# Attention in units of one head pair and 512 queries, with the weighing of two half steps issued together

## The chip, the cores and the metric

The kernel runs on one core of one Trainium2 chip. The metric is the device time of one execution in microseconds (us). TensorE (PE) multiplies matrices into PSUM, VectorE (DVE) and ScalarE (ACT) read and write PSUM and SBUF, GpSimd (POOL) works on SBUF, SyncE (SP) mostly issues DMAs. Each engine works through its own instructions in order and meets the others at semaphores.

## The reference, cut to what matters

The program is two transformer layers on x of 4 x 1024 x 256: a state-space mixer, a mixture of experts with top 2 of 8, an attention, and a gated feed-forward part with blockwise fp4 quantisation, each followed by a layer norm. The change touches only the attention of the second layer:

```python
qkv = (zn @ W_qkv + b_qkv).reshape(b, n, 3, H, DH)     # b=4, n=1024, H=16, DH=16
scores = jnp.einsum('bhqd,bhkd->bhqk', q, k) * scale   # 1024 x 1024 for each of 16 heads
attn = jax.nn.softmax(scores, axis=-1)
msa = jnp.einsum('bhqk,bhkd->bhqd', attn, v)
```

## The kernel before, in words

The first part of the program (mixer, experts) takes some 470 us. After it a function `sequence(b, more)` on every engine does attention, projection and feed-forward of one batch entry, four times, with the first steps of entry b+1 laid into the end of entry b.

Attention works on pairs of heads (NP = 8 pairs; the two heads of a pair, a = 0 and 1, sit on partitions 0.. and 64.. of `Qs` and `Ks`, so that their matmuls address different rows of the PE array). The scores are computed twice, in float32r from split high and low parts:

- **For the maxima.** `score_max(n)` (L976) is one matmul of 48 rows, 128 queries by 512 keys, into one PSUM bank; DVE's `row_maxima` (L1536) reduces the bank to a maximum for each query. A pair takes UN = 32 such units (8 query tiles, 2 key halves, 2 heads). Banks: six take turns in the first UN units of an entry, afterwards only the three banks 4, 5, 6, and a unit waits on `sld` until the previous user of its bank has been read. When a pair's 32 units are reduced, DVE's `negated_maxima` makes the negated maxima, split in two (three small operations, L1540 to L1542), PE turns them (`turn_max`, L983, in a bank slot of its own), DVE copies them to `MR` (L1549), and SP sends them by two DMAs (`maxima_row`, L440) to two extra rows of `Qs` (flow `mrow`). These rows, against rows of ones in `Ks`, subtract the maximum inside the second product. `turn_slot(p)` puts the turn SOON = 1 unit (first pair) or LATER = 4 units after the pair's last.
- **For the weights.** A half step n is one key tile (128 keys) and 512 queries of both heads: `transposed_scores` (L1006, two matmuls of 50 rows by 512 columns into two banks), ACT's exponential to `Pb` (L708), and `weigh` (L1019, four fp32 matmuls with 32 output columns each, eight matmul instructions, accumulating in bank 7). A step m = (pair, key tile kt) holds the half steps qh = 0 and 1; an entry has 64 steps, 128 half steps. After a pair ACT copies bank 7 out (`evac_o`, L681; flow `ov` frees the bank).

PE's order is written out by hand. It issues the 32 units of the first pair, between them the eight `values` products (L960) with the filler matmuls of `keep_warm` (L1028), 25 further fillers, the turn, and six units of the second pair (START = 6). Then comes the loop over m. In it `maxima(upto)` keeps the units ahead of the half steps: `ahead = UN + min(LEAD + 4*m, START + 5*m)`, that is five units a step for the first steps and then four. For steps 12 to 52 (`apart`) each half step is

```python
maxima(ahead + 2 * qh + 1)
transposed_scores(p, kt, qh)
maxima(ahead + (2 if not qh else step if apart else 3))
if apart:
    weigh(m - 1, qh)
```

so one `weigh` stands behind each half step. In the steps before 12 and from 53 (LAST) on, the two `weigh` of a step stand together behind its second half step; in the steps before 12 one unit follows them, and from 53 on no units are left.

SP sends the stacked high and low parts of a pair (`stack(p)`, twelve DMAs, L432; flow `stk`) and the rows of maxima in one fixed order: stacks 0, 1, 2, row 0, stack 3, then row p-3 and stack p for p = 4 to 7, then the last rows. After the last unit DVE goes on to sums for the following stage (`combine` of the next entry), and reads the heads' results (`rc`, L1586) when PE has turned them.

Of the kernel before, what the change touches and what calls it, by code (L numbers as in the profile page):

```python
# [7 lines left out]
F32 = mybir.dt.float32  # L8
# [24 lines left out]
LEAD, START = 12, 6  # L33
# [49 lines left out]
def transformer(nc, xT, state_cols, WtT, WbT, Wc4, WoT, Dv, bo, sel, Wg, W1, b1, W2, b2, rev,  # L83
                lnw_d, lnb_d, Wqkv, bqkv_d, Wproj, bproj, w_gate, w_up, w_down, ident_d, out):
    ctx = ExitStack()
    with ctx:
# [90 lines left out]
        NM = sb("NM", [P, 2, TT])  # L177
        NMs = sb("NMs", [P, 2, 2, TT], F32R)
        MR = sb("MR", [4 * TT, 2, P], F32R)
# [58 lines left out]
        def h_dram(name, shape):  # L238
# [20 lines left out]
        UN = 2 * TT * 2  # L259
        SLOTS = NP * UN + NP  # L260
# [4 lines left out]
            qkp=8, qka=8, qkv=8, vp=TT, vv=TT, **{f"stk{k}": NP // NB * STK - (0 if k else KST) for k in range(NB)}, kst=KST, mrow=16 * 2 * NP,  # L265
            slp=SLOTS, sld=SLOTS, nms=NP,
# [6 lines left out]
        CHAIN, AHEAD = 132, 13  # L273
# [12 lines left out]
        def turn_slot(p):  # L286

            if p + 1 == NP:
                return SLOTS - 1
            return UN * (p + 1) + (LATER if p else SOON) + p  # L290

        def slot_bank(i):

            return (4, 5, 6, 0, 1, 2)[i % 6] if i < UN else 4 + (i - UN) % 3

# [42 lines left out]
        def _(sp):  # L338
# [76 lines left out]
            for b in range(B):  # L415
# [18 lines left out]
                def maxima_row(p):  # L434
                    F["sld"].wait(sp, b, turn_slot(p) + 1)
                    if p >= NB:
                        F["bp"].wait(sp, b, 2 * KT * (p - NB + 1))
                    for a in range(2):
                        r, at = ROW * a + STACK, 2 * a * TT
                        F["mrow"].inc(sp.dma_start(  # L440
                            Qs[r:r + 2, p % NB, :].rearrange("o (t q) -> o t q", t=TT).bitcast(F32),
                            MR[at:at + 2 * TT, p % 2, :].bitcast(F32)), by=16)
# [8 lines left out]
                for p in range(NP - NB + 1, NP):  # L451
                    maxima_row(p)
# [113 lines left out]
        def _(act):  # L566
# [110 lines left out]
            def sequence(b, more):  # L677
# [23 lines left out]
                for p in range(NP):  # L701
                    for kt in range(KT):
                        for qh in range(2):
                            n = 2 * (KT * p + kt) + qh
                            F["bp"].wait(act, b, n + 1)
                            if n >= 4:
                                F["pv"].wait(act, b, n - 3)
                            F["ex"].inc(act.activation(Pb[:, kt % 2, 2 * qh:2 * qh + 2, :],  # L708
                                                       PS[:, 2 * qh:2 * qh + 2, :], ACT.Exp, scale=0.25))
                            if kt == 0 and p > 0 and qh == 0:  # L710
                                evac_o(p - 1)
# [74 lines left out]
        def _(pe):  # L786
# [163 lines left out]
            def sequence(b, more):  # L950
# [13 lines left out]
                def score_max(n):  # L964

                    p, r = n // UN, n % UN
# [12 lines left out]
                def turn_max(p):  # L979
                    i = turn_slot(p)  # L980
                    F["nms"].wait(pe, b, p + 1)
                    F["sld"].wait(pe, b, slot_free(i))
                    F["slp"].inc(pe.transpose(PS[0:4 * TT, slot_bank(i), 0:P],  # L983
                                              NMs[:, :, :, :].rearrange("p a k t -> p (a k t)").bitcast(F32), ident[:, :]))
# [3 lines left out]
                def maxima(upto):  # L988

                    while issued[0] < min(upto, NP * UN):  # L990
# [8 lines left out]
                def transposed_scores(p, kt, qh):  # L999

                    n = 2 * (KT * p + kt) + qh
                    if n >= 2:
                        F["ex"].wait(pe, b, n - 1)
                    for a in (1, 0):
                        rows = slice(ROW * a, ROW * a + MROWS)
                        ins = pe.matmul(PS[:, 2 * qh + a, :], Ks[rows, p % NB, kt * P:(kt + 1) * P],  # L1006
# [3 lines left out]
                def weigh(m, qh):  # L1010

                    p, kt = m // KT, m % KT
                    if kt == 0 and p:
                        F["ov"].wait(pe, b, p)
                    F["ex"].wait(pe, b, 2 * m + qh + 1)
                    for c in range(2):
                        for a in range(2):
                            j = 2 * a + c
                            ins = pe.matmul(PS[32 * j:32 * j + 32, 7, qh * QW:(qh + 1) * QW], V[:, kt, 2 * p + a, :],  # L1019
                                            Pb[:, kt % 2, 2 * qh + a, c * QW:(c + 1) * QW],  # L1020
                                            start=(kt == 0 and qh == 0), stop=(kt == KT - 1), skip_group_check=True)
# [7 lines left out]

                maxima(3)  # L1030
# [18 lines left out]
                FIRST = 12  # L1049
                LAST = (NP * UN - UN - LEAD) // 4  # L1050
                for m in range(NP * KT):
                    p, kt = m // KT, m % KT
                    if kt == 0:
                        F["mrow"].wait(pe, b, 16 * 2 * (p + 1))
                    ahead = UN + min(LEAD + 4 * m, START + 5 * m)
                    step = UN + min(LEAD + 4 * (m + 1), START + 5 * (m + 1)) - ahead
                    apart = FIRST <= m < LAST
                    for qh in range(2):
                        if apart:
                            maxima(ahead + 2 * qh + 1)  # L1060
                        transposed_scores(p, kt, qh)
                        maxima(ahead + (2 if not qh else step if apart else 3))
                        if apart:
                            weigh(m - 1, qh)
                    if not apart:
                        for qh in range(2 if m else 0):
                            weigh(m - 1, qh)
                        maxima(ahead + step)
                        if m == LAST:
                            turn_max(NP - 1)  # L1070
                for qh in range(2):
                    weigh(NP * KT - 1, qh)
# [115 lines left out]
        def _(dve):  # L1188
# [307 lines left out]
            def sequence(b, more):  # L1496
# [33 lines left out]
                def row_maxima(lo, hi):  # L1530
                    for n in range(lo, hi):
                        p, r = n // UN, n % UN
# [5 lines left out]
                def negated_maxima(p):  # L1538
                    F["sld"].wait(dve, b, unit_slot(UN * (p + 1) - 1) + 1)
                    link(dve.tensor_reduce(NM[:, :, :], MX[:, p % 2, :, :, :], AX.X, ALU.max, negate=True))  # L1540
# [3 lines left out]
                def maxima_rows(p):  # L1544
                    i = turn_slot(p)
                    F["slp"].wait(dve, b, i + 1)
                    if p >= 2:
                        F["mrow"].wait(dve, b, 16 * 2 * (p - 1))
                    F["sld"].inc(dve.tensor_copy(MR[:, p % 2, :], PS[0:4 * TT, slot_bank(i), 0:P]))  # L1549

                row_maxima(0, UN)
                for p in range(NP):
                    negated_maxima(p)
                    gap = LATER if p else SOON
                    if p + 1 < NP:
# [170 lines left out]
```

How the kernel before makes its waits and increments, by code:

```python
    def wait(self, eng, b, n, ahead=0):  # L65
        eng.wait_ge(self.sem, b * self.per + (ahead * self.per + n))
# [12 lines left out]
    def wait(self, eng, n):  # L79
        eng.wait_ge(self.sem, n)
# [256 lines left out]
        @block.sync  # L337
# [18 lines left out]
            load(lnw[:, :], lnw_d, s_late)  # L356
            load(lnb[:, :], lnb_d, s_late)
            load(wqkv[:, :, :], Wqkv.rearrange("(c p) n -> p c n", p=P), s_late)
            load(bqkv[:, :], bqkv_d, s_late)
            load(wproj[:, :, :], Wproj.rearrange("(c p) n -> p c n", p=P), s_late)
            load(bproj_sb[:, :], bproj.to_broadcast([P, D]), s_late)
            def load_ffn(w, src):
                sp.dma_start(WN[w], src.rearrange("(t p) k -> p t k", p=WP if w < 2 else P)).then_inc(s_wld[w], 16)
            for b in range(B):
                sp.wait_ge(C["xn"].sem, TT * (b + 1))
                C[f"mid{b % 2}"].inc(sp.dma_start(x_mid[b * S:(b + 1) * S, :].rearrange("(t p) d -> p t d", p=P), Xa[b % 2]), by=16)
            sp.wait_ge(C["tab"].sem, 1)
            def load_w1(k):
                e = sp.value_load(tab[0:1, k:k + 1], min_val=0, max_val=E - 1)
                if k >= 2:
                    sp.wait_ge(C["wl"].sem, k - 1)
                C["w1a" if k % 2 == 0 else "w1b"].inc(sp.dma_start(
                    W1t[k % 2], W1[bass.ds(e, 1), :, :].rearrange("o (c p) n -> p (o c) n", p=P)), by=16)
                return e
# [1 line left out]
            def load_w2(k, e):  # L378
                if k >= 2:
                    sp.wait_ge(C["yp"].sem, SA * (k - 1))
                if k == 0:
```

## Time and profile before

| | |
|---|---|
| time of three runs | 1770.61 us median (1768.52 to 1770.95) |
| span of the profiled execution | 1760.0 us |
| median of the runs less that span | 10.6 us |
| busy: PE, DVE, ACT, POOL | 91%, 76%, 50%, 15% |
| mean granted TensorE clock | 0.948 |
| costliest groups | L1536 DVE 635.3 us, L708 ACT 511.1, L976 PE 389.8, L1006 PE 341.0, L1019 PE 319.0 |
| attention of one entry, first reduction to last copy of bank 7 | 196.5 to 199.3 us, four times |

The profile comes from one further execution; its total device time is not listed apart from its span, so the time outside the span is taken from the median of the runs. Matmuls are pipelined and overlap, so a PE that is busy in the profile is not PE at its peak, and a group's busy time counts overlaps twice. The granted clock is 1.00 (2.4 GHz) or 0.50 (1.2 GHz); a value between the two in a stretch is a mixture of both in time.

### The profile page before, as it was taken

How to read it: one execution, taken by the hardware profiler on the slowest of the kernel's cores; microseconds unless marked ns; L12 is line 12 of the kernel's file. 1: busy time of each engine (PE TensorE's matmuls, PEld its weight loads, DVE VectorE, ACT ScalarE, POOL GpSimd, SP SyncE). 2: the span in 40 equal slices, each digit the busy share in tenths (PEclk: the TensorE clock that was granted, in tenths of full speed). 3: DMA queues.
4: the chain of work that ended last, by engine and by line, in shares of the span. 5: the costliest groups of instructions: out<-in, count | busy, mean ns of one | idle time of the engine just before them, and what ended most of it. 6: DMA issues, size and time to landing. Idle time of an engine off the chain costs nothing.

```text
span 1760.0 us, 27981 instructions
## 1 busy us (share of the span) xinstructions
PE 1597.9 (91%) x10698; PEld 962.5 (55%) x10698; DVE 1345.8 (76%) x2629; ACT 875.5 (50%) x1294; POOL 258.6 (15%) x255
## 2 busy tenths in 40 slices
PE   5988999994799998899999989999997999999895
PEld 2757899994343336565433556543345754333664
DVE  3675555542589996888999689889968987996686
ACT  1313444441347784252677624367782344778412
POOL 0144223223100120210003030100203010000120
PEclk8988999997789999998999989999999998999998
DMA  3127878774312310013222000412300032210000
GB/s 134 48 72 220 253 250 257 247 235 146 60 27 36 71 38 1 1 25 73 38 38 74 2 0 1 89 27 39 80 14 1 1 78 36 36 24 2 1 0 24
DMA packets 80175, 123.03 MB, mean 70 GB/s; under 512 B 13530, under 2 KB 55771, under 8 KB 80043
## 3 DMA queue, kind: packets, MB, share of 16 engines
q1 hardware_dynamic: 70666, 93.46, 20.5%
q0 software_dynamic: 9376, 27.80, 5.4%
q8 instruction: 85, 1.39, 0.3%
q14 instruction: 48, 0.39, 0.1%
HBM read 76.84 MB, written 18.61 MB: 54 GB/s over the span
## 4 chain that ended last, share of the span: by engine, by line
PE 76%; DVE 13%; ACT 4%; issue 3%; DMA 1%; POOL 1%; SPq 1%; DVEq 0%; ACTq 0%; POOLq 0%
PE PS L1019 15%; PE PS L976 13%; PE PS L901 7%; PE PS L1131 7%; PE PS L889 6%; PE PS L1006 6%; PE PS L1141 5%; DVE MX L1536 3%; PE PS L946 3%; PE PS L960 2%; ACT Pb L708 2%; PE PS L839 2%; PE PS L1028 1%; PE PS L1090 1%; PE PS L1167 1%
## 5 line engine op out<-in xcount | busy, mean ns | idle before, releaser
L1536 DVE TENSOR_REDUCE MX<-PS 128x1 f32<-128x512 f32 x1024 | 635.3, 683 | 43.2 <-PE PS L976 41.2
L708 ACT ACTIVATE Pb<-PS 128x1024 f32<-128x1024 f32 x512 | 511.1, 1026 | 174.7 <-PE PS L1006 174.5
L976 PE MATMUL PS<-Ks,Qs 48*128 48x512 f32 x1024 | 389.8, 472 | 7.1 <-DVE MX L1536 4.3
L1006 PE MATMUL PS<-Qs,Ks 50*128 50x512 f32 x1024 | 341.0, 464 | 14.3 <-ACT Pb L708 11.5
L1019 PE MATMUL PS<-Pb,V 128*32 128x256 f32 x4096 | 319.0, 401 | 1.0
L976 PEld LDWEIGHTS PS<-Ks,Qs 48*128 48x128 f32 x1024 | 163.6, 191 | 218.8 <-DVE MX L1536 174.4
L1019 PEld LDWEIGHTS PS<-Pb,V 128*32 128x32 f32 x4096 | 92.3, 110 | 163.2 <-ACT Pb L708 84.5
L1006 PEld LDWEIGHTS PS<-Qs,Ks 50*128 50x128 f32 x1024 | 140.2, 191 | 49.7 <-ACT Pb L708 36.1
L901 PE MATMUL PS<-Pb,OT 128*128 128x256 f32 x624 | 141.0, 379 | 0.0
L889 PE MATMUL PS<-Ks,Qs 128*128 128x256 f32 x936 | 127.5, 294 | 6.4 <-DVE Ks L1416 6.4
L889 PEld LDWEIGHTS PS<-Ks,Qs 128*128 128x128 f32 x936 | 119.7, 197 | 8.9 <-DVE Ks L1416 7.8
L901 PEld LDWEIGHTS PS<-Pb,OT 128*128 128x128 f32 x624 | 115.6, 190 | 14.2
L1131 PE MATMUL PS<-wgT,XT 128*128 128x352 f32 x256 | 95.8, 525 | 15.3 <-DVE OT L1634 12.3
L473 POOL DMA_INDIRECT OT<-x_mid,idx x78 | 79.5, 1020 | 197.8 <-PE PS L878 160.0
L621 ACT ACTIVATE Qs<-Pb 128x1024 fp32r<-128x1024 f32 x39 | 41.3, 1060 | 121.3 <-DMA Pb<-W 121.3
L1141 PE MATMUL PS<-wdT,Pb 128*128 128x256 f32 (+1 forms) x384 | 96.2, 393 | 2.0 <-ACT Pb L761 2.0
L1141 PEld LDWEIGHTS PS<-wdT,Pb 128*128 128x128 f32 (+1 forms) x384 | 70.8, 192 | 26.9 <-issue 11.6
L632 ACT ACTIVATE OT<-PS,b1t 128x256 f32<-128x256 f32 x156 | 64.7, 470 | 38.2 <-PE PS L889 38.0
L1131 PE MATMUL PS<-wuT,XT 128*128 128x352 f32 x256 | 81.1, 460 | 0.0
L1131 PEld LDWEIGHTS PS<-wgT,XT 128*128 128x128 f32 x256 | 53.1, 218 | 43.6 <-DVE OT L1634 13.3
L738 ACT ACTIVATE OT<-PS 128x704 f32<-128x704 f32 x32 | 24.2, 756 | 103.4 <-PE PS L1131 103.4
L1412 DVE TENSOR_TENSOR Qs<-Pb,Qs 128x1024 fp32r<-128x1024 f32 x39 | 47.7, 1224 | 30.3 <-ACT Qs L621 29.9
(286 smaller groups left out, 1893.9 us busy)
## 6 DMA issues: line engine op xcount, KB each, us to landing
Pb<-W SPq DMA_DIRECT2D x78, 512.0 KB, 4.3
y_slot<-V SPq DMA_DIRECT2D x39, 256.0 KB, 3.9
Qs<-Qh SPq DMA_DIRECT2D x128, 64.0 KB, 2.3
Ks<-Kh SPq DMA_DIRECT2D x120, 64.0 KB, 2.3
V<-b SPq DMA_DIRECT2D x39, 128.0 KB, 3.5
XT<-x_mid POOLq DMA_DIRECT2D x4, 1024.0 KB, 6.2
out<-Pb POOLq DMA_DIRECT2D x4, 1024.0 KB, 6.7
OT<-xT SPq DMA_DIRECT2D x2, 1024.0 KB, 6.4
```

The costliest lines, as they stand in the source:

```text
L473: C[("xa", "xb", "xc")[k % 3]].inc(pool.indirect_dma_start(Xm[k % 3][:, a, :], None, x_mid[:, :], bass.IndirectOffsetOnAxis(idx[:, SA * k ...
L632: C["hr"].inc(act.activation(HTm[k % 2][:, hc, :], PS[:, 2 + 2 * (k % 2) + hc // 2, hc % 2 * ST:(hc % 2 + 1) * ST], ACT.Relu, bias=b1t[:, ...
L708: F["ex"].inc(act.activation(Pb[:, kt % 2, 2 * qh:2 * qh + 2, :], PS[:, 2 * qh:2 * qh + 2, :], ACT.Exp, scale=0.25))
L889: ins = pe.matmul(PS[:, 2 + 2 * (k % 2) + hc // 2, hc % 2 * ST:(hc % 2 + 1) * ST], w[k % 2][:, c, hc * P:(hc + 1) * P], x[k % 2][:, c, :], ...
L901: ins = pe.matmul(PS[:, 6 + k % 2, a * D:(a + 1) * D], HTm[k % 2][:, hc, a * P:(a + 1) * P], W2t[k % 2][:, hc, :], start=(hc == 0), stop=( ...
L946: ins = pe.matmul(o, wqkv[:, kc, w * D + c * P:w * D + (c + 1) * P], tokens, start=(kc == 0), stop=(kc == DC - 1))
L976: F["slp"].inc(pe.matmul(PS[:, slot_bank(i), :], Qs[rows, p % NB, t * P:(t + 1) * P], Ks[rows, p % NB, kh * HALF:(kh + 1) * HALF], start=T ...
L1006: ins = pe.matmul(PS[:, 2 * qh + a, :], Ks[rows, p % NB, kt * P:(kt + 1) * P], Qs[rows, p % NB, qh * HALF:(qh + 1) * HALF], start=True, st ...
L1019: ins = pe.matmul(PS[32 * j:32 * j + 32, 7, qh * QW:(qh + 1) * QW], V[:, kt, 2 * p + a, :], Pb[:, kt % 2, 2 * qh + a, c * QW:(c + 1) * QW] ...
L1131: ins = pe.matmul(PS[:, 2 * w + a, 0:IH], XT[:, c, t * P:(t + 1) * P], wT[:, c, a * IH:(a + 1) * IH], start=(c == 0), stop=(c == DC - 1))
L1141: ins = pe.matmul(PS[:, 6 + t % 2, 0:D], HT[0:k, c, :], wdT[0:k, c, :], start=(c == 0), stop=(c == IC - 1))
L1536: F["sld"].inc(dve.tensor_reduce(MX[:, p % 2, a, t, kh:kh + 1], PS[:, slot_bank(i), :], AX.X, ALU.max))
```

## The change

The unit of work becomes one pair and one half of the queries. UN falls from 32 to 16 and there are NU = 16 such groups u = (pair, qh). Negated maxima, turn, copy and the DMAs of the rows are done for each u, on half as many elements. `mrow` becomes two flows, one for each half. The half steps run in the order pair, query half, key tile: n = 8u + kt, so the first half step needs the maxima of 16 units only. The filler matmuls are fewer: none between the first `values` and few after them, but three times two (`fill`) behind the first three half steps. START is 8. The loop runs over half steps; each issues one unit ahead of the second product and the rest behind it, and the `weigh` of half steps n-3 and n-2 stand together behind every odd n. The last rows' turn stands ahead of half step LAST + 2. ACT copies bank 7 out behind the exponential n % 16 == 1 instead of n % 16 == 0. DVE's chain of small operations grows by 16 links an entry.

```diff
-LEAD, START = 12, 6
+LEAD, START = 12, 8
-        UN = 2 * TT * 2
-        SLOTS = NP * UN + NP
+        UN = 2 * TT
+        NU = 2 * NP
+        QT = TT // 2
+        SLOTS = NU * UN + NU
...
-                for p in range(NB - 1):
+                stack(0)
+                stack(1)
+                maxima_row(0)
+                for p in range(2, NB):
                     stack(p)
-                maxima_row(0)
-                stack(NB - 1)
+                    maxima_row(p - 1)
                 for p in range(NB, NP):
-                    maxima_row(p - NB + 1)
+                    for u in range(2 * (p - NB) + NB - 1, 2 * (p - NB) + NB + 1):
+                        maxima_row(u)
                     stack(p)
...
+                for n in range(NU * KT):                                  # ACT
+                    F["bp"].wait(act, b, n + 1)
+                    if n >= 4:
+                        F["pv"].wait(act, b, n - 3)
+                    F["ex"].inc(act.activation(weights_of(n), PS[:, 2 * (n % 2):2 * (n % 2) + 2, :], ACT.Exp, scale=0.25))
+                    if n > 2 and n % (2 * KT) == 1:
+                        evac_o(n // (2 * KT) - 1)
...
-                for t in range(1, TT):                                    # PE
-                    maxima(4 * t + 1)
-                    F["vv"].wait(pe, b, t)
-                    keep_warm(2, 1)
-                    maxima(4 * t + 3)
+                for t in range(1, 5):
+                    maxima(3 * t + 3)
                     values(t)
                 maxima(UN)
+                for t in (5, 6):
+                    values(t)
+                maxima(UN + SOON)
+                values(7)
                 F["vv"].wait(pe, b, TT)
-                keep_warm(18)
-                maxima(UN + SOON)
-                keep_warm(7, 1)
+                keep_warm(2, 1)
                 for n in range(SOON, START):
                     maxima(UN + n + 1)
                     keep_warm(3, (n + 1) % 2)
...
+                ahead = lambda n: UN + min(LEAD + 2 * n, START + 5 * n // 2)
+                LAST = (NU * UN - UN - LEAD) // 2
+                for n in range(NU * KT):
+                    if n == LAST + 2:
+                        turn_max(NU - 1)
+                    maxima(ahead(n) + 1)
+                    transposed_scores(n)
+                    maxima(ahead(n + 1))
+                    if n < 3:
+                        fill(2)
+                    elif n % 2:
+                        weigh(n - 3)
+                        weigh(n - 2)
+                for n in range(NU * KT - 2, NU * KT):
+                    weigh(n)
...
+                for u in range(NU):                                       # DVE
+                    negated_maxima(u)
+                    gap = LATER if u else SOON
+                    if u + 1 < NU:
+                        row_maxima(UN * (u + 1), UN * (u + 1) + gap)
+                    maxima_rows(u)
+                    if u + 1 < NU:
+                        row_maxima(UN * (u + 1) + gap, UN * (u + 2))
```

## Rows read from the trace of the kernel before

**Rows 1.** Windows of the four attentions, reductions alone: stretch; length, busy (count), clock, DMA
```profile
472.94:671.05 198.11, 158.84 (x256) 0.97 0.22 44
793.13:992.43 199.30, 158.83 (x256) 0.96 0.23 48
1116.20:1312.70 196.50, 158.77 (x256) 0.97 0.23 49
1434.78:1633.94 199.16, 158.81 (x256) 0.96 0.18 33
```

**Rows 2.** Chain of waits, two weigh together: start, duration, engine and line
```profile
522.56 1.00 PE PS L1019 x16
523.56 0.44 PE PS L976
524.02 0.70 DVE MX L1536
524.77 0.50 PE PS L976
525.27 1.00 PE PS L1019 x16
```

**Rows 3.** Chain of waits, one weigh behind each half step
```profile
560.15 0.57 PE PS L1019 x8
560.72 0.43 PE PS L976
561.14 0.24 PE PS L1006 x2
```

**Rows 4.** Timeline of the second entry's start: start, duration, instruction [idle before <-releaser]
```profile
799.09 1.13 PE L960 MATMUL PS<-wqkv,XT 128*128 128x256 f32 x4
...
812.39 0.19 DVE L1540 TENSOR_REDUCE NM<-MX 128x16 f32<-128x32 f32 x1
...
812.91 0.68 DVE L1536 TENSOR_REDUCE MX<-PS 128x1 f32<-128x512 f32 x1
...
813.43 0.29 PE L983 MATMUL PS<-ident,NMs 128*32 128x128 f32 x1
...
814.18 3.08 DVE L1536 TENSOR_REDUCE MX<-PS 128x1 f32<-128x512 f32 x5
...
816.87 0.50 PE L1006 MATMUL PS<-Qs,Ks 50*128 50x512 f32 x2 [0.62 <-DMA Qs<-MR]
```

**Rows 5.** Timeline at a pair's end with two weigh together
```profile
529.03 0.60 ACT L681 ACTIVATE OT<-PS 128x512 f32<-128x512 f32 x1 [1.04 <-PE PS L1019]
```

**Rows 6.** Windows of PE behind the first second products: length, busy (count), clock, DMA
```profile
496.70:500.10 3.40, 2.89 (x14) 1.00 0.61 102
500.10:513.80 13.70, 13.70 (x75) 0.50 0.18 31
821.00:838.10 17.10, 17.10 (x96) 0.50 0.12 20
1138.50:1141.90 3.40, 2.47 (x16) 0.99 0.45 76
1141.90:1152.10 10.20, 10.10 (x54) 0.50 0.31 53
1462.70:1479.80 17.10, 17.10 (x96) 0.50 0.14 23
```

**Rows 7.** Chain of waits at the lower clock
```profile
501.39 1.86 PE PS L1019 x16
...
506.15 1.86 PE PS L1019 x16
```

**Rows 8.** Chain of waits when no units are left
```profile
657.13 1.00 PE PS L1019 x16
...
661.09 1.00 PE PS L1019 x16
```

**Rows 9.** Timeline of DVE at the first entry's end
```profile
672.83 0.26 DVE L1586 RECIPROCAL rc<-PS 128x16 f32<-128x16 f32 x1 [9.24 <-PE PS L1080]
```

More of the change, by code:

```diff
@@ L264, in transformer @@
             ve=1, rs=2, nm=1, vel=2, rsl=4, nml=2, zn=TT, xn=1, xw=TT, xa=TT - 2 + TT // 2, xd=2 + TT // 2, x2=1, vm=1, trp=4 + 2, xt=4 + 2, xl=TT - 3,
-            qkp=8, qka=8, qkv=8, vp=TT, vv=TT, **{f"stk{k}": NP // NB * STK - (0 if k else KST) for k in range(NB)}, kst=KST, mrow=16 * 2 * NP,
-            slp=SLOTS, sld=SLOTS, nms=NP,
+            qkp=8, qka=8, qkv=8, vp=TT, vv=TT, **{f"stk{k}": NP // NB * STK - (0 if k else KST) for k in range(NB)}, kst=KST, mrow0=16 * 2 * NU // 2, mrow1=16 * 2 * NU // 2,
+            slp=SLOTS, sld=SLOTS, nms=NU,
             bp=2 * KT * NP, ex=2 * KT * NP, pv=2 * KT * NP, ov=NP,
@@ L700, in sequence @@
                                                ACT.Copy))
[L701 to L711, printed above, removed]
+                for n in range(NU * KT):
[5 more added lines that the diff above has]
+                        evac_o(n // (2 * KT) - 1)
                 evac_o(NP - 1)
@@ L988, in maxima @@
                 def maxima(upto):
-                    while issued[0] < min(upto, NP * UN):
+                    while issued[0] < min(upto, NU * UN):
                         n = issued[0]
@@ L1005, in transposed_scores, with weigh @@
                         rows = slice(ROW * a, ROW * a + MROWS)
-                        ins = pe.matmul(PS[:, 2 * qh + a, :], Ks[rows, p % NB, kt * P:(kt + 1) * P],
+                        ins = pe.matmul(PS[:, 2 * (n % 2) + a, :], Ks[rows, p % NB, kt * P:(kt + 1) * P],
                                         Qs[rows, p % NB, qh * HALF:(qh + 1) * HALF], start=True, stop=True)
                     F["bp"].inc(ins)
-                def weigh(m, qh):
-                    p, kt = m // KT, m % KT
-                    if kt == 0 and p:
+                def weigh(n):
+                    u, kt = n // KT, n % KT
+                    p, qh = u // 2, u % 2
+                    if kt == 0 and qh == 0 and p:
                         F["ov"].wait(pe, b, p)
-                    F["ex"].wait(pe, b, 2 * m + qh + 1)
+                    F["ex"].wait(pe, b, n + 1)
                     for c in range(2):
@@ L1028, in keep_warm, with fill @@
                         pe.matmul(PS[:, 3 if at else 7, :], Qs[at:at + STACK, 0, 0:P], Ks[at:at + STACK, 0, 0:HALF], start=True, stop=True)
+                def fill(n):
+                    for _ in range(n):
+                        pe.matmul(PS[:, 7, :], Qs[0:STACK, 0, 0:P], Ks[0:STACK, 0, 0:HALF], start=True, stop=True)
                 maxima(3)
@@ L1048, in sequence @@
                 F["vm"].wait(pe, b, 1)
[L1049 to L1072, printed above, removed]
+                ahead = lambda n: UN + min(LEAD + 2 * n, START + 5 * n // 2)
[13 more added lines that the diff above has]
+                    weigh(n)
                 F["ov"].wait(pe, b, NP)
```

81 lines of the change are left out of this document (40 added, 41 removed).

## The prediction

> **What bounds the kernel now.** Read first the windows of the four attentions [rows 1]. They last 198.1, 199.3, 196.5 and 199.2 us, mean 198.3, together 793 of 1760 us; the change touches nothing else. In each DVE's 256 reductions are busy for 158.8 us. Back to back they follow one another at (3.08 - 0.68)/4 = 0.60 us [rows 4], so they need 154 us; the rest of an attention is where DVE waits for PE, and a tail without units.
>
> Next the chain of waits in three modes. With both `weigh` together (half steps 12 to 23) a loop closes through DVE and PE: 16 weighing matmuls 1.00 us, the unit behind them and its semaphore 0.44, its reduction 0.70, the unit that takes the freed bank 0.50, and weighing again; from 522.56 to 525.27 that is 2.70 us for two half steps and four units [rows 2]. The loop passes one reduction, though DVE would need only 4 x 0.60 = 2.40. With one `weigh` behind each half step (24 to 105) the chain holds PE alone, 0.57 + 0.43 + 0.24 = 1.24 us a half step, 2.48 for two [rows 3]. Behind the last unit the chain runs through products, weighing and exponential at (661.09 - 657.13)/4 = 0.99 us a half step [rows 8].
>
> Last the granted clock. It falls to 1.2 GHz in all four entries, in the first of them 500.1 - 496.7 = 3.4 us after the first second product, for 13.7, 17.1, 10.2 and 17.1 us, 14.5 on average [rows 6]. There two half steps take 506.15 - 501.39 = 4.76 us [rows 7] and PE is busy throughout.
>
> **The change, part by part.** Times are from an entry's first reduction. Units count from 0.
>
> *Start.* Before, the first second product comes at 816.87 - 793.13 = 23.7 us, behind 32 units and the rows of maxima [rows 1, 4]. Now 16 units do: 16 x 0.60 = 9.6, and the negated maxima 812.91 - 812.39 = 0.52 [rows 4]. The products of values, though, lie thicker: behind the sixteenth unit PE has values 5, 6, one unit, value 7, ACT's copy of it and two fillers before the turn. Four matmul instructions of a value take 1.13 us [rows 4], the three some 3.3, with unit and copy 4.3; PE's lead is some four and a half reductions and the small operations, about 3.3. So I let DVE stand still for 1.0 (between 0 and 2): the reduction of unit 17 starts at 12.0, that of 21 at 14.4. It ends at 15.1 and frees the bank of unit 24, the last that PE issues before the first second product. The rows are there by then: from the turn at 11.3 by 816.87 - 813.43 = 3.44 [rows 4] makes 14.7. First second product: 15.1, 8.6 earlier than before.
>
> *The first eight half steps* issue five units for two. The first `weigh` follows unit 33, whose bank is free when unit 30 has been reduced: 12.0 + 13 x 0.60 + 0.68 = 20.5 (0.68 is one reduction, [rows 4]); with 0.50 to the weighing and 1.00 in it [rows 2] half step 4 stands at 22.0. By the same loop plus one further reduction two half steps take 2.70 + 0.60 = 3.3, and those with the first boundary 3.9: half step 8 at 29.1 to 29.2, at the full clock.
>
> *Steady state.* The order is now unit, product, unit, unit, product, unit, weigh, weigh. Turned round by one place that is the order of rows 2, with the same three banks. The mode at 2.48 us is gone, and everything from half step 8 to 114 (LAST) runs at 2.70: 53 x 2.70 = 143.1. A price below 2.40 is excluded by DVE, and nothing in the loop makes it longer than 2.7 to 2.9; I take the row.
>
> *Boundaries.* There are 16 instead of 8 of them, 13 in this stretch. The negated maxima (0.52, and the last reduction before them keeps 0.11 of its overlap) fall where DVE is idle for 2.70 - 2.40 = 0.3: some 0.35 remain in the loop. The turn stands directly behind the weighing and pushes the next unit by some 0.22 of its 0.29 [rows 4], and DVE's copy fits into its idle time: together 0.57, I take 0.60 (none if the idle time hid all, 0.95 if it hid nothing). 13 x 0.60 = 7.8. The copy of bank 7 costs nothing any more: before, ACT stood for 1.04 us in front of it with a product ready [rows 5]; now one more exponential comes first and fills that time.
>
> So half step 114 stands at 29.1 + 143.1 + 7.8 = 180.0.
>
> *Tail.* 14 half steps instead of 22 remain behind the last unit: 14 x 0.99 = 13.9, and 1.5 for the last two `weigh`: 195.4. DVE's work for the next stage stays hidden: it had 9.24 us to spare [rows 9], of which 8 x 0.99 = 7.9 go with the shorter tail and some 0.9 with the later turn. If it were late, that is 0 to 1 us an entry.
>
> *SP and POOL.* SP sends 32 small DMAs an entry instead of 16. A row has 8 units, 5.4 us, from its turn to its product and needs 3.44 [rows 4]. Stack 2 now stands behind row 0 and stack 3 behind row 1, both with over 20 us to spare; POOL's gathers hang on a count of `weigh` that is reached earlier. I take 0, and bound it by 2 us in an entry.
>
> *Sum at the full clock:* 195.4 against 198.3, 2.9 us an entry, 11.5 in all: 1759. Of the 8.6 us that the start gains, most go back to the slower steady state: 0.22 for each of 41 pairs of half steps, and four more pairs that ran at 2 x 0.99.
>
> *The clock.* Before it fell, PE issued no weighing; the stretches hold 14 and 16 matmuls in 3.4 us [rows 6]. Now the first `weigh` starts 21.0 - 15.1 = 5.9 us behind the first second product instead of 501.39 - 496.70 = 4.7 [rows 6, 7], with 8 second products, 10 units and 6 fillers: 24 matmuls in 5.9 us, or 14 in 3.4, as in the stretch ahead of the first fall. The fillers make the first half denser than the second, so the clock need not fall each time. A fall costs the share 1 - 3.0/4.76 = 0.37 of 14.5 us, 5.4 us (3.0 is the mean of 3.9, 3.3 and 2.7). I take three falls of four: 16.2. Sum: -11.5 + 16.2 = +4.7, on the median 1770.6 + 4.7 = **1775.3 us**. The profiled execution has 1760.0 of span and I leave the 10.6 us around it alone.
>
> A rule of the Trainium skill speaks for this change: "Changing tiling mode (not just tile) drains the TensorE" (TensorEngine Tiling (Array Packing), Key Properties). Two `weigh` together have half the changes between the tiles of 128 x 32 and of 64 x 128. The trace agrees on the price, 2 x 0.57 = 1.14 us of weighing apart against 1.00 together, but by rows 2 PE's saving does not come out, since the loop through DVE is longer. By the rule alone the steady state would be DVE's.
>
> **The rivals.**
> - *The clock holds (faster).* The six fillers, in the first 4 us, are enough in three or four entries: 1759 to 1765. For it: two matmuls for each half step where the clock fell; against it: the count above.
> - *Grouping pays.* The loop is not the one of rows 2, and DVE alone sets the pace: 2.40 a pair of half steps, boundaries at their full 0.72. Per entry 53 x 0.30 - 13 x 0.12 = 14.3 less, 57 in all: about 1718. Only the rule above speaks for it; rows 2 against it.
> - *The boundaries cost more.* Twice as many rows, and each must be through DVE, PE, DVE, SP and a DMA before its product. At 0.95 on DVE and a wait of 0.5 us for each of 16 rows: 13 x 0.35 + 8 = 12.6 an entry, 50 in all, at the worst; a third of it gives 1792. The 2.0 us of slack speak against it. It decides from 5.4 us between turn and product on.
> - *The change does not bring its earlier start.* PE is late with values and turn, DVE stands 4 us more at the start: 4 x 4 = 16 more, 1791. Rows 4 give 1.0.
> - *No change that can be measured:* two falls, -11.5 + 10.8, 1770.
>
> **How the numbers follow.** Forecast (three or four falls, 1775 to 1781) 0.40; two falls 0.12; clock holds 0.24; grouping pays 0.05; boundaries 0.13; start 0.06. Three runs of before differ by 0.14%, so 0.2%, 3.5 us, is about what can be told from no change. Faster: 0.24 + 0.05 + 0.03 from uncertain sums near two falls = 0.32. Within: 0.09 of two falls and 0.12 of the forecast's lower part = 0.21. Slower: 0.47. Range: 1757 (clock holds, loop a little shorter) to 1790; outside stay grouping pays, and the upper parts of boundaries and start. The forecast's own range is 1768 to 1784.
>
> **What would show it.** First reduction to first second product 15 us (right from 14 to 16). Half steps in the steady state in pairs of 2.70, and DVE idle for 0.2 to 0.3 before one reduction in four; at 2.40 to 2.50 the loop is wrong. Sixteen half steps in 22.8 us instead of 21.2. No wait of ACT in front of L681. From last reduction to last copy of bank 7 some 15.5 us instead of 23.6. The granted clock 0.5 in three of four entries, 4 to 6 us behind the first second product; at 1.00 throughout the time is below 1765. A wait on the DMA of a row at other places than the first would speak for the boundaries. I would be wrong in kind if the steady state were faster than before, or the clock had held and the time were still higher.

## The result, and the profile after

| | before | after |
|---|---|---|
| time, median of 8 runs each on one chip | 1772.33 us (1764.84 to 1776.81) | 1782.67 us (1778.86 to 1787.08) |
| ratio, with its 95% interval | | 1.0064 [1.004, 1.0087] |
| profiled execution: its own time, span | | 1782.49 us, 1780.7 us |
| mean granted clock of that execution | 0.948 | 0.94 |
| chain that ended last: PE, DVE | 76%, 13% | 64%, 26% |

The change makes the kernel slower by 0.64%, 11.3 us on 1772.3. The forecast was 4.7 us slower, at 1775.3 us; the direction and the range held, more than half of the size was missing. Executions more than 1.5% above the fastest of their kernel are left out of every ratio here.

The windows of the four attentions, which answer to [rows 1], are read first (start:end, length, busy and count, granted clock, DMA share, GB/s; the reductions alone). An entry is one of the four batch entries, 0 to 3:

```profile
473.43:678.84 205.41, 158.71 (x256) 0.94 0.21 42
802.62:1009.43 206.81, 158.75 (x256) 0.93 0.22 46
1133.20:1338.42 205.22, 158.75 (x256) 0.94 0.22 47
1460.50:1655.26 194.76, 158.34 (x256) 1.00 0.18 34
```

DVE's busy time is what it was, 158.7 us. Together the four last 812.2 us instead of 793.1, 19.1 more of the 20.7 by which the two profiled spans differ, so the loss lies in the attentions. Three of them are near 206 and one is at 194.8, with its clock at 1.00. That spread asks for two explanations, one for the plain entry and one for what came on top of it.

The chain of waits (start, duration, what) shows the plain part, with a stretch of the steady state in the first entry, and at its end what happened 40 us later ("..." marks rows left out):

```profile
561.40 1.00 PE PS L1029 x16
...
565.39 0.18 DVE NM L1546
...
567.12 1.00 PE PS L1029 x16
568.12 0.21 PE PS L989
...
570.03 1.00 PE PS L1029 x16
571.03 0.44 PE PS L982
571.47 0.02 issue
571.50 0.70 DVE MX L1541
572.20 0.04 issue
572.24 0.50 PE PS L982
572.74 1.00 PE PS L1029 x16
...
613.68 0.29 DVE MR L1555
613.97 0.02 issue
613.99 0.67 SPq L447
614.65 0.04 issue
614.69 4.98 DMA Qs<-MR
619.67 0.71 issue
620.38 0.50 PE PS L1015 x2
```

From weighing at 570.03 to weighing at 572.74 lie 2.71 us: the loop of [rows 2], link for link, now everywhere. From 561.40 to 567.12 is the one boundary of that stretch with its negated maxima, and the turn (L989) stands behind the weighing that follows. Behind the last "..." the chain leaves this loop: PE waits for the row of maxima of the twelfth group, which SP sends at 613.99 and which takes 4.98 us to land. The timeline of POOL at that moment (start, duration, engine, line, instruction, [idle before <-releaser]) says what it landed beside:

```profile
613.86 0.93 POOL L492 DMA_DIRECT2D XT<-x_mid  x1 [143.67 <-DMA Ks<-Kl]
...
615.29 1.04 POOL L502 DMA_INDIRECT Qh<-y_slot,posb  x1 [0.17 <-issue]
```

POOL had stood for 143.67 us in front of L492, a fetch of 1 MB for the stage after, until the last stack had landed, and was released 0.13 us ahead of the row's DMA.

The row's landing at 619.67 was not the end of it. By the chain PE resumed only 0.71 us later, and ACT and DVE resumed later still (timeline):

```profile
620.72 0.40 PE L982 MATMUL PS<-Ks,Qs 48*128 48x512 f32 x2
...
622.41 2.12 DVE L1541 TENSOR_REDUCE MX<-PS 128x1 f32<-128x512 f32 x3 [3.11 <-PE PS L982]
622.45 1.02 ACT L715 ACTIVATE Pb<-PS 128x1024 f32<-128x1024 f32 x1 [3.46 <-PE PS L1015]
```

Both units had ended by 621.12, and DVE started 1.3 us after that. The same lateness of 1.0 to 1.3 us stands at half step 88 in entries 1 and 2, and nowhere in the profile of before. Its cause is open; it comes back below on the second chip.

The last view is of PE alone, in the stretches of the attentions in which the clock fell:

```profile
493.40:503.60 10.20, 10.16 (x56) 0.50 0.27 45
623.10:636.80 13.70, 13.64 (x74) 0.50 0.24 69
821.10:827.90 6.80, 6.80 (x35) 0.50 0.42 68
950.80:964.40 13.60, 13.56 (x74) 0.50 0.23 69
974.70:981.50 6.80, 6.80 (x44) 0.50 0.02 4
1152.20:1172.70 20.50, 20.46 (x111) 0.50 0.34 57
1285.30:1288.70 3.40, 3.40 (x24) 0.50 0.38 106
```

The first, third and sixth are behind the first second products of entries 0, 1 and 2, and answer to [rows 6]. The other four have no counterpart in the profile of before. Three of them begin 0.4 to 0.7 us behind the start of the exponential of half step 88, for which PE had waited, in the middle of entries 0 to 2; the one at 974.70 follows 24 us behind such a fall. Entry 3, behind which no entry is fetched, has neither the wait nor such a fall.

An entry's sum by steps, from its first reduction, needs three instants. A half step "stands" at the start of its exponential. Half step 8 stands at 33.0, 31.6, 34.7 and 30.4 us in the four entries, half step 80 at 135.0, 133.6, 137.7 and 132.3, half step 104 at 176.9, 178.5, 176.8 and 166.3. Against the last entry the first three thus lose 2.7, 1.2 and 5.4 us ahead of half step 80 (9.3 together) and 8.0, 11.0 and 5.1 from 80 to 104 (24.1 together); behind that they run alike. Of the 24.1 us, 2.7, 2.6 and 2.6 are lost from 80 to 88, while the granted clock is still 1.00: that is the wait with the late resumption. The other 16.1 us come from 88 to 104, with the clock at 0.50 for part of it.

### The profile page after: what moved, and what is told of

Its sections match the earlier page's. It is cut to its first block, busy times and chain, and to the rows that moved or that the text cites. A ratio compares the mean times of both kernels' runs of the same rounds, so it can differ in the third digit from the quotient of the medians.

```text
span 1780.7 us, 28121 instructions
## 1 busy us (share of the span) xinstructions
PE 1600.7 (90%) x10630; PEld 1010.8 (57%) x10630; DVE 1370.7 (77%) x2757; ACT 865.3 (49%) x1294; POOL 256.5 (14%) x255
## 4 chain that ended last, share of the span: by engine, by line
PE 64%; DVE 26%; issue 4%; ACT 3%; DMA 2%; SPq 0%; POOL 0%; DVEq 0%; ACTq 0%; POOLq 0%
DVE MX L1541 14%; PE PS L1029 11%; PE PS L982 11%; PE PS L907 7%; PE PS L1136 7%; PE PS L895 6%; PE PS L1146 5%; PE PS L952 3%; PE PS L966 2%; PE PS L1015 2%; PE PS L845 2%; PE PS L1095 1%; PE PS L1172 1%; ACT Pb L715 1%; PE PS L884 1%
## 5 line engine op out<-in xcount | busy, mean ns | idle before, releaser
L715 ACT ACTIVATE Pb<-PS 128x1024 f32<-128x1024 f32 x512 | 497.8, 1022 | 245.9 <-PE PS L1015 240.8
L982 PEld LDWEIGHTS PS<-Ks,Qs 48*128 48x128 f32 x1024 | 178.1, 192 | 257.4 <-DVE MX L1541 202.0
L1015 PE MATMUL PS<-Qs,Ks 50*128 50x512 f32 x1024 | 316.1, 445 | 4.1 <-issue 1.8
L1029 PE MATMUL PS<-Pb,V 128*32 128x256 f32 x4096 | 287.5, 400 | 0.7
L1015 PEld LDWEIGHTS PS<-Qs,Ks 50*128 50x128 f32 x1024 | 164.7, 194 | 27.6 <-ACT Pb L715 15.8
L1029 PEld LDWEIGHTS PS<-Pb,V 128*32 128x32 f32 x4096 | 109.5, 112 | 115.8 <-issue 60.4
L1136 PE MATMUL PS<-wgT,XT 128*128 128x352 f32 x256 | 99.4, 540 | 15.3 <-DVE OT L1640 12.3
```

The costliest lines, as they stand in the source:

```text
L715: F["ex"].inc(act.activation(weights_of(n), PS[:, 2 * (n % 2):2 * (n % 2) + 2, :], ACT.Exp, scale=0.25))
L982: F["slp"].inc(pe.matmul(PS[:, slot_bank(i), :], Qs[rows, p % NB, t * P:(t + 1) * P], Ks[rows, p % NB, kh * HALF:(kh + 1) * HALF], start=T ...
L1015: ins = pe.matmul(PS[:, 2 * (n % 2) + a, :], Ks[rows, p % NB, kt * P:(kt + 1) * P], Qs[rows, p % NB, qh * HALF:(qh + 1) * HALF], start=Tru ...
L1136: ins = pe.matmul(PS[:, 2 * w + a, 0:IH], XT[:, c, t * P:(t + 1) * P], wT[:, c, a * IH:(a + 1) * IH], start=(c == 0), stop=(c == DC - 1))
```

## The experiments

There were twelve runs on three chips, with the kernel before beside them every time. Its median was 1756.2 us on the first chip (the first four runs), 1777.4 on the second (the next four) and 1758.9 or 1755.3 on the third, so only ratios go from one chip to another. The chip of the first comparison is not on record; its 1772.3 us for the kernel before lie near the second's. The theory was: in an undisturbed entry grouping costs what the loop of [rows 2] costs and the earlier start pays for it; on top come the falls of the clock at the start, and the fetch that meets the twelfth row. The first rival was that the late wait is a small matter, and its time that of the clock alone.

**SP's order.** Stack p goes out between the two rows instead of behind both, so that the last stack lands earlier and the fetch with it:

```diff
-                    for u in range(2 * (p - NB) + NB - 1, 2 * (p - NB) + NB + 1):
-                        maxima_row(u)
+                    maxima_row(2 * (p - NB) + NB - 1)
                     ...
+                    maxima_row(2 * (p - NB) + NB)
```

> The changed kernel, with SP's order turned in one place: for p = 4 to 7 row 2p-5, stack p, row 2p-4 instead of both rows and then the stack. Theory (late pile-up): in the changed kernel POOL waits on the last stack, which now leaves SP one row later, so its fetch of 1 MB and its first eight gathers fall together at half steps 86 to 90; the row for half step 88 then takes 4.98 us to land instead of some 2, PE stands, and the clock falls in the middle of the attention. With the stack one row earlier, the fetch comes some eight half steps earlier, the gathers are spread as before, half steps 86 to 94 of the first three entries take 2.7 a pair and the granted clock stays at 1.00 from half step 16 to the end. Entries of 195 to 198 us instead of 205 to 207; the whole 23 to 30 us faster than the changed kernel: 1755 to 1762, which is 0.990 to 0.994 of the kernel before. Rival (density): the grouped order at 2.70 us is too thin to keep the clock and the fall in mid-attention comes anyway somewhere; then the time stays within 8 us of 1783, ratio 1.002 to 1.008.

Measured 1.0043 [1.002, 1.0066]. In the first two entries the wait is gone: every eight half steps from 8 to 120 but the last take 11.33 us. In the third the fetch, now earlier, meets the row before (of half step 80), by POOL's timeline and the chain:

```profile
1243.70 0.90 POOL L492 DMA_DIRECT2D XT<-x_mid  x1 [124.58 <-DMA Ks<-Kl]
...
1244.59 5.47 DMA Qs<-MR
```

PE stands there, half steps 72 to 88 take 24.6 us instead of 22.7, and the clock falls for 3.4 us from 1250.3 on. So the edit moved the meeting in one entry of the three and did not remove it. The entries last 197.5, 195.7, 200.9 and 200.3 us, 794.3 together, 18 fewer than after; yet the time missed its expectation by far, which had put the late wait at over 1% of the time. At the start the clock fell in all four entries here, for 47.8 us together, against three entries and 37.5 us in the profile of after.

**The fetch alone.** POOL issues the fetch of 1 MB before it waits for the last stack, and the gathers stay behind that wait:

```diff
-                    F[f"stk{NB - 1}"].wait(pool, b, NP // NB * STK)
                     ...
+                    F[f"stk{NB - 1}"].wait(pool, b, NP // NB * STK)
```

> The changed kernel, with POOL's fetch of the next entry's 1 MB put ahead of its wait for the last stack; the gathers keep their place. If the fetch of 1 MB is what delays the row of half step 88, the wait there is gone and entries 0 to 2 last 195 to 198 us, 1755 to 1762 in all. If it is the eight gathers in a row, the row still takes over 4 us to land, half steps 86 to 88 still take over 4 us, and the time stays at 1778 to 1785.

Measured 1.0076 [1.0044, 1.0107]. Half steps 80 to 104 run at 11.33 us for eight in all entries though the gathers still start when the last stack has landed: the fetch delays the row, not the gathers. But now the fetch meets the entry's first row, and the first second product comes at 19.1, 19.5 and 19.5 us in entries 0 to 2 instead of 15.8. The timeline of the first entry:

```profile
487.33 0.93 POOL L492 DMA_DIRECT2D XT<-x_mid  x1 [14.87 <-ACT V L709]
488.14 1.37 SPq L447 DMA_DIRECT2D Qs<-MR  x2
494.78 0.79 PE L1015 MATMUL PS<-Qs,Ks 50*128 50x512 f32 x2 [2.83 <-DMA Qs<-MR]
```

The same fetch in another place makes the same small transfer late by 3.3 to 3.7 us.

**Weighing apart from half step 24 on.** One `weigh` stands behind each even half step too, as the kernel before had it:

```diff
+                    elif 24 <= n < LAST:
+                        weigh(n - 2)
```

> The changed kernel with one weigh (of half step n-2) behind each half step from 24 to 113, as the kernel before has it, everything else as changed. Theory (loop): the pair of half steps costs 2.70 because 1.00 us of weighing stands between two units; apart it is 2.48 and PE alone in the chain. With boundaries at 0.6 to 0.8 sixteen half steps take 21.3 to 21.8 instead of 22.7, 5 to 8 us an entry, so 20 to 32 us less than the changed kernel: 1751 to 1763, ratio 0.988 to 0.995, the late pile-up still in it. Rival (boundaries): with 16 boundaries the steady state is set by them and not by the weighing; then sixteen half steps stay at 22.4 or more and the gain is under 6 us.

Measured 0.9897 [0.9853, 0.9941], as expected (the entries last 190.7 to 196.0 us). The chain holds PE alone again, with 1.24 us from weighing to weighing, as in [rows 3]:

```profile
560.27 0.57 PE PS L1029 x8
560.84 0.43 PE PS L982
561.27 0.24 PE PS L1015 x2
...
561.51 0.57 PE PS L1029 x8
```

Eight half steps take 10.83 us instead of 11.33. Over the 90 half steps from 24 to 114 that is 5.6 us an entry, 22.5 in all, 1.3% for one edit. The ratios say 1.7% beside after's 1.0064 and 1.3% beside the 1.0025 measured further below; neither is known to be from this chip. In entries 1 and 2 the twelfth row is late here too (12.0 and 11.5 us from 80 to 88), and no clock falls behind it.

**The kernel before, grouped throughout.** Nothing of the change but its grouping:

```diff
-                FIRST = 12
+                FIRST = NP * KT
```

> The kernel before with both weigh together in all steps (the apart mode never entered), nothing else changed. Theory (loop): 41 steps at 2.70 instead of 2.48 and seven copies of bank 7 with a stall of 0.66 instead of 0.45: 0.22 x 41 + 7 x 0.2 less what the smaller boundaries give back (5 x 0.1) = 9.9 us an entry, 40 in all: 1812, ratio 1.018 to 1.026. Rival: if the grouping saved PE time that counts, the time would stay or fall, ratio under 1.005.

Measured 1.0219 [1.018, 1.0259]: sixteen half steps take 22.9 us instead of 21.2 (11.48 + 11.41). Grouping thus costs in both loops, 1.7 us for sixteen half steps in the old one and 2 x 0.5 = 1.0 in the new one. The rival "grouping pays" falls by both runs.

**Both edits, order and weighing apart.**

> The changed kernel with both single edits at once: SP's order turned (stack p between the two rows) and one weigh behind each half step from 24 to 113. Theory: the edits are independent. The apart mode alone gave 0.990, with 10.84 us for eight half steps instead of 11.33; SP's order takes the pile-up of 1 MB and one row away, which cost the apart mode only 2 to 4 us an execution. Expected ratio 0.983 to 0.989. Rival: SP's order bought its time in the clock alone, and the apart mode keeps the clock by itself; then nothing is added and the ratio stays at 0.990.

Measured 0.9967 [0.9935, 1.0], on the second chip; missed. From half step 24 to 72 the eight take 10.83 us as they should, and to 80 too, but for the third entry, where the fetch meets a row again. From 80 to 104 entries 0 to 2 need 11.6 to 14.1 us for eight, in just the stretch in which POOL gathers for the next entry, and entry 3 needs 10.83. The next run is the kernel before on this same chip.

**The kernel before, once more, on the second chip.**

> The kernel before, unchanged, for a profile beside those of the other kernels. Expected: attentions of 196 to 200 us with a fall of the clock behind the first second product in all four. If its clock falls are shorter or fewer than in the first profile, that explains why the changed kernel with SP's order, whose four attentions sum to 794 us against 793 in the first profile, still measured 1.0043.

Measured 1784.72 us, with the same trouble: half steps 80 to 104 take 34.8 us in its first entry and 31.6 in its last. So it does not belong to the change. In that phase DVE and ACT resume late behind a matmul that is finished by the records, by 0.6 to 1.6 us. All four kernels profiled on this chip show it, and none on the first and third, where the same step is never over 0.5 us late; why is open. It is what the first profile of after shows at half step 88. The clock falls in the middle of entries here too, for 10.2 and 20.5 us in entries 1 and 2, although no row is late in the kernel before.

**Other fillers.** Each pair of the fillers of 48 rows is replaced by one fp32 matmul of 128 rows, beside the new order of SP:

```diff
-                    for _ in range(n):
-                        pe.matmul(PS[:, 7, :], Qs[0:STACK, 0, 0:P], Ks[0:STACK, 0, 0:HALF], start=True, stop=True)
+                    for _ in range(n // 2):
+                        pe.matmul(PS[:, 7, 0:D], XT[:, 0, 0:P], wqkv[:, 0, 2 * D:3 * D], start=True, stop=True)
```

> The changed kernel with SP's order turned, and with each pair of fillers behind the first three half steps (two float32r matmuls of 48 rows and 512 columns) replaced by one fp32 matmul of 128 rows and 256 columns, which takes the same time of PE (two instructions of 0.21 us). Theory (clock): the fall at the start of an entry comes from what PE does ahead of it, and it costs 2.5 to 7 us an entry; with fillers of 128 rows the clock holds in three or four entries, half step 8 stands at 29 to 31 us instead of 31 to 35, all entries last 194 to 197 us, and the time is 8 to 16 us below that with SP's order alone (ratio 0.994 to 0.999 of before, against 1.0043). Rival: the clock falls for another reason, then entries of 195 to 201 us and the ratio of 1.004 stay.

Measured 0.9938 [0.991, 0.9967], at the edge of the expectation; with the second chip's late phase entries 0 to 2 last 198.7 to 202.6 us and not 194 to 197. The windows of PE from an entry's first reduction to half step 8 answer the question of the start. First the kernel with SP's order alone (on the first chip), then this one:

```profile
475.83:508.88 33.05, 32.37 (x171) 0.85 0.31 52
...
1436.09:1470.78 34.69, 34.07 (x171) 0.77 0.40 82
```

```profile
474.16:504.59 30.43, 29.33 (x171) 1.00 0.31 51
...
1442.77:1473.16 30.39, 29.30 (x171) 1.00 0.37 81
```

The count of matmul records is the same; the clock stays at 2.4 GHz four times out of four where it fell four times out of four, and half step 8 comes at 30.4 us. The same holds on one chip for two kernels that differ in the fillers alone: with both other edits and the old fillers ("Both edits" above) these windows have clocks of 0.89, 0.84, 0.80 and 0.80, with the new ones ("All three edits" below) 1.00 four times. The Trainium skill (TensorE: Matmul & The Clock Gate, What's actually happening) says that the gate acts on how busy PE has been lately. By its rows PE is busy for 98% of the first window above and for 96% of the one that keeps its clock, so the busy time of the profile does not tell the one from the other.

**All three edits.**

> The changed kernel with all three: SP's order, weigh apart from 24 to 113, fillers of 128 rows. Theory: the three add up: entries of 189 to 191 us, 25 to 35 us less than the kernel before, ratio 0.976 to 0.984. Rival (clock has another cause): as the kernel with the two edits.

Measured 0.9845 [0.98, 0.9891], a hair above the expected 0.976 to 0.984, with the second chip's late phase in it: the entries last 205.1, 193.9, 195.6 and 189.4 us, the first with one low clock of 34 us in that phase.

**After, and SP's order, once more side by side.** These two runs ask for the late wait's price, on the third chip.

> The changed kernel once more, beside the kernel with SP's order turned on one and the same chip, since the two were compared with the kernel before on different chips so far (1.0064 and 1.0043) and their profiles differ by more (four attentions of 812 and 794 us). Theory (pile-up): SP's order is worth 12 to 20 us, 0.7 to 1.1%: the changed kernel stands at 1.004 to 1.012 here, with rows of half step 88 that land after 4 to 5 us in entries 0 to 2. Rival: the pile-up is an affair of one execution and the two kernels agree within 0.3%.

> The changed kernel with SP's order turned, beside the unchanged changed kernel. Theory: 0.993 to 0.999 times the kernel before where the changed one stands at 1.004 to 1.012. Rival: within 0.3% of the changed kernel.

Measured 1.0025 [1.0001, 1.0049] for after and 1.005 [1.0026, 1.0075] with the other order: the theory missed, its rival held. The meeting of row and fetch is there in after, the row's DMA takes 5.56 us, by the chain and POOL's timeline:

```profile
616.67 5.56 DMA Qs<-MR
```

```profile
615.80 0.93 POOL L492 DMA_DIRECT2D XT<-x_mid  x1 [141.83 <-DMA Ks<-Kl]
```

Half steps 80 to 88 take 12.43, 12.60 and 11.92 us instead of 11.33, so it costs 0.6 to 1.3 us an entry, and no clock falls behind it. ACT resumes 0.05 us behind its product here, where the first profile had over 1 us. The windows of the attentions of after on this chip, the first and the last of four:

```profile
477.20:673.84 196.64, 158.61 (x256) 0.99 0.22 44
...
1442.64:1642.75 200.11, 158.62 (x256) 0.95 0.18 33
```

The two between last 198.4 and 200.7 us; with the other order of SP the four last 195.7, 199.0, 200.9 and 194.9.

By itself the wait is thus worth some 3 us of the whole, less than these intervals, and SP's order can't be told from none (its third entry has a late row here too). What made it dear in the first profile of after were the late resumption of PE, ACT and DVE and the falls of the clock behind it.

**Weighing apart from half step 8 on,** with the other two edits (`elif 8 <= n < LAST`).

> All three edits (SP's order, one weigh behind each half step, fillers of 128 rows), with the apart mode from half step 8 on instead of 24. Eight more pairs at 2.48 instead of 2.70 us: 1.8 us an entry, 7 in all, on the 0.9845 of the kernel with apart from 24: ratio 0.976 to 0.984, half step 24 at 51.3 to 51.7 us instead of 53.1. Rival: the clock falls again behind half step 8 without the grouped mode, then no gain.

Measured 0.9812 [0.9779, 0.9845], 1726.06 us beside 1758.87: the best of all, faster than both kernels. Half step 24 stands at 52.1 us, expected 51.3 to 51.7. The first of its attentions:

```profile
475.36:663.89 188.53, 159.29 (x256) 1.00 0.23 46
```

The other three last 188.5, 189.5 and 188.6 us, and no clock falls in any. Its five runs lie within 1.9 us, while the twelve of after on the same chip spread over 18.0 (1755.3 to 1773.3). That fits a clock that no longer falls at random inside the attentions, but only one of the five was profiled. In its third entry a row is late as well (half steps 72 to 80 take 11.6 us instead of 10.8), and the clock holds.

**Before, with the same two helps.** The fp32 filler behind its first three half steps, and weighing apart from step 4 on (FIRST = 4). This asks what the units of 512 queries are worth by themselves.

> The kernel before (whole pairs as units, 32 units before the first second product), given what the best kernel has besides its units: one fp32 filler of 128 rows behind each of the first three half steps, and one weigh behind each half step from 8 instead of 24. It asks what the units of 512 queries themselves are worth: with them that kernel has entries of 188.5 us and 0.9812. Theory (the start pays, less its boundaries and tail): the earlier start is worth 8.0 us, the eight fewer half steps in the tail 8 x (1.08 - 0.99 - ...) near nothing, since each half step leaves the tail at 0.99 and enters the steady state at 1.35, 8 x 0.36 = 2.9 back, and eight more boundaries give back 8 x 0.35 = 2.8; so this kernel has entries of 190.5 to 193 us and a ratio of 0.984 to 0.991. Rival (clock and weigh do it all): entries of 188 to 189.5 us and a ratio within 0.003 of 0.981.

Measured 1.0004 [0.9976, 1.0031]; missed, its clock still falls. The profiled execution took 1772.2 us, 13.8 above this kernel's median. In the two entries between those shown the clock fell for 44.4 and 27.3 us, from 46 us behind the first reduction on, and they last 211.1 and 204.6 us; no fall touched these:

```profile
474.44:667.90 193.46, 159.21 (x256) 1.00 0.23 45
...
1451.56:1644.95 193.39, 159.21 (x256) 1.00 0.18 34
```

Between 193.4 and 188.5 lie 4.9 us an entry: that is what the units of 512 queries are worth (the earlier start and the shorter tail, net of eight more boundaries) when both kernels weigh apart and hold their clock. The two also differ in the order of SP and in the fillers ahead of the first second product, which were not tried singly.

## Why the prediction was right in direction and short in size

*The start: right, 0.7 late.* First second product at 15.8 us in all entries, forecast 15.1, before 23.7. The first weighing follows 6.0 us behind it in the first entry, forecast 5.9; both are rows of PE:

```profile
489.23 0.71 PE L1015 MATMUL PS<-Qs,Ks 50*128 50x512 f32 x2
...
495.23 1.94 PE L1029 MATMUL PS<-Pb,V 128*32 128x256 f32 x16
```

Half step 8 at the full clock stands at 30.4, forecast 29.1.

*The steady state: right.* 2.71 us a pair of half steps, row for row (forecast 2.70). Together with the boundaries, sixteen half steps take 22.66 us, forecast 22.8; a boundary costs 22.66 / 2 - 4 x 2.71 = 0.49, forecast 0.60. Weighing apart in the changed kernel and weighing together in the kernel before confirmed that this mode is where the start's gain goes. The rule on changes of the tiling mode was rightly set aside: two groups apart do take 0.14 us more of PE than one, and the loop through DVE hides it.

*The tail: right.* From the last reduction's end to the last copy, 179.86 to 194.76 from the entry's start, 14.9 us; forecast 15.4, before 23.6. Half step 114 stands at 180.2, forecast 180.0. DVE's reserve of 9.24 us [rows 9] has shrunk to 0.54, forecast some 0.5:

```profile
680.62 0.26 DVE L1592 RECIPROCAL rc<-PS 128x16 f32<-128x16 f32 x1 [0.54 <-PE PS L1085]
```

The plain entry is thus 194.8 us, forecast 195.4. Four of them make 779.0, 14.0 below [rows 1]; I had 11.5.

*The clock at the start: right in number by luck, and too dear.* Three entries of four fell, as forecast, for 10.2, 6.8 and 20.5 us. They cost 9.3 us together where I had put 3 x 5.4 = 16.2. In the other profiled executions with these fillers three or four fell. The reason that I gave does not hold. I had counted 14 matmuls in 3.4 us, as sparse as before. Between the first second product and the fall PE had 22 in 4.2 us, busy for 4.09 (2.60 of 2.70 and 3.12 of 3.22 in the other two entries), against 2.89 of 3.40 before; it was denser and its clock fell all the same. What decides is open. On the third chip the forecast came near (1.0025, that is 4.4 us) by another such sum: -14.0, 14.1 for four falls and 2.7 for the late wait make 2.8.

*SP and POOL: this step failed.* "I take 0, and bound it by 2 us in an entry." I followed SP's queue to the rows and the stacks, and saw the gathers "reached earlier", but not that the last stack, now two rows and not one behind, is what POOL waits for in front of its fetch of 1 MB. On the third chip the wait's own cost stayed within the bound (0.6 to 1.3 us an entry). In the first profile it was 2.6 to 2.7 us, above it, with PE, ACT and DVE late behind what had released them. On top came falls of the clock in the middle of an entry, where I had looked for them only at the start: with the wait 8.0, 11.0 and 5.1 us, 24.1 in that execution. -14.0 + 9.3 + 24.1 is the 19.1 measured, to 0.3.

Without this term the sum would have been -14.0 + 9.3 = -4.7, a faster kernel. So the direction, too, came out right in that profile by a term that I had put at nothing.

Whether the wait brings the fall about is not shown. For it speaks that a fall follows at once in three entries of the first profile, in one with SP's order alone and in one with all three edits. Against it stand the three entries of the third chip and two of the kernel that weighs apart, which waited and did not fall, and the kernel before on the second chip, which had no late row and fell twice. The lateness of ACT and DVE is a second suspect; in the first profile the two came together, and no run tells them apart there.

*The base: wrong.* I left "the 10.6 us around the span alone". The profiled execution of after has 1782.49 - 1780.7 = 1.8 us around its span. If before had as little, its profiled execution took some 1762 us, and the 10.6 were mostly that it was a quick one, which [rows 1] could not show. A sum made against it compares a quick execution of before with a typical one of after. The eight runs of each kernel beside each other, 10.3 us apart, are the measure; the two profiles, 20.7 apart, are not.

*The rivals.* "Grouping pays" and "the start does not come" are excluded by rows. "The boundaries cost more" had the right kind of fault, a row that its product waits for, but the wrong reason: not the number of rows, but one row of sixteen that meets a large transfer. The sign named for it, a wait on a row at another place than the first, was there. "The clock holds" was a matter of the fillers, and with other fillers it came true at the start.

## What to carry to other kernels

When a step in an issue queue is moved, follow every engine that waits for what it sends, down to the first large transfer behind that wait, and ask which small transfer with a reader will be on its way at that moment. A mode that halves the switches of PE was worth nothing here, since the chain ran through another engine; read the chain in both modes before grouping. Where the clock falls at random, the kernels differ in how often it does: compare medians of many runs, read the mechanism from entries without a fall, and price the falls apart. Where an engine starts late behind work that is finished by the records, count that time by itself before it is put down to the step in front of it.

## What the runs showed of the hardware

- The two small DMAs of a row (4 KB each), issued by SP 0.13 and 0.17 us behind a fetch of 1 MB by POOL, landed after 4.98 and 5.56 us, and the first row's product came 3.3 to 3.7 us late when its DMAs stood 0.8 us behind the fetch. Undisturbed, by the chain of the kernel before at its first row, the same step took 1.92 with twice the bytes:

```profile
494.64 1.92 DMA Qs<-MR
```

  By the Trainium skill (DMA: Bandwidth & Descriptors, Queues, rings and completion order) a DMA engine takes turns between its queues packet by packet. Being on another queue did not protect the row here; whether packets alternated, no row here shows.
- With fillers of 128 rows in fp32 instead of 48 rows in float32r, of nearly the same time, the clock stood at 2.4 GHz up to half step 8 of every entry in the four kernels that had them; in those without them it fell there in three or four entries of four. What the chip counts is not settled by this: rows and type were changed together.
- Three chips gave the kernel before medians of 1756, 1777 and 1755 to 1759 us. On the one at 1777 DVE and ACT came 0.6 to 1.6 us late again and again while POOL's gathers ran, and so they did by 1.0 to 1.3 us in the first profile of after. The fourth entry, behind which nothing is fetched or gathered, does not show it in any of the profiles. The cause is open; no kernel without gathers was tried.
